# State of a Mamba block in two head halves, its two products as tile pairs of the matmul array

## The chip, the cores and the metric

The program runs on one core of a Trainium2 chip, as one launch. The metric is the device time of that launch in microseconds (us). A core has a matmul engine (TensorE, PE in the profile, with PEld for its weight loads), a vector engine (VectorE, DVE), a scalar engine (ScalarE, ACT), GpSimd (POOL) and a queue that issues transfers (SyncE, SP). They run on their own and wait for each other by semaphores.

## What is computed

Three blocks in a row on 4096 tokens of 256 features: a mixture of experts, a Mamba-2 block, and the same mixture of experts again. The change is in the middle block. Cut to what matters there:

```
zxbcdt = x @ W_in                       # x: layer-normed, (2, 2048, 256)
dt = softplus(dt + dt_bias)             # 8 heads
xBC = silu(conv(xBC) + conv_b)          # causal, 4 taps; x_ssm 8 heads x 64, B 64, C 64
dA = exp(dt * -exp(A_log))
def step(s, inp):                       # s: (batch, 8 heads, 64, 64)
    s = s * dA_t[..., None, None] + dt_t * x_t * B_t
    y = einsum('bhpn,bn->bhp', s, C_t)
    return s, y
y = y + D * x_ssm
y = y * silu(z)
y = y * rsqrt(mean(y * y) + eps) * norm_weight
return y @ W_out
```

## The kernel before

The outer blocks (`ffn_block`, run twice) sort tokens by expert with indirect transfers and are untouched. The middle block is `mamba_block`. It cuts the 4096 tokens into 32 chunks of 128 (T = 32; GC = 4 chunks make a group, 16 chunks make a batch entry). The recurrence is done chunk by chunk: inside a chunk by products with a masked decay matrix, between chunks through a state S.

The order on every engine is written out by hand as a loop over slots, `for s in SLOTS`. In slot s, chunk s gets its state products, chunk s+1 its decay matrix and transposes, chunk s+2 its z projection, chunks s+8 and s+9 their first steps, and chunks s-1 to s-3 their last. Below, "slot i" is the slot in which chunk i gets its state products. Slots differ by k = i mod 4, since the convolution and the softplus of a group of four chunks are laid into certain slots (tables `EARLY`, `LATE`, `TAPPED`, `HANDED`): with k = 3 DVE does the softplus chain of a group ahead, with k = 0 the cumulative sums are made, and with k = 0, 1 and 2 DVE has convolution taps to do. Chunks 28 to 31 have nothing ahead of them.

The steps that the change and the prediction touch, in the order of a slot, with their lines:

- `from_state` (PE, L1323): y from the state, the product of C transposed (CT, 64 partitions by 128 tokens, the weights) with S (64 partitions by 512 columns, 8 heads x 64), into PSUM bank pS. Every fp32 product becomes two weight loads and two matmul instructions on PE ("x2" in the timeline).
- `scale_state` (DVE, L1630): pS times the decay since the chunk's start, into yv.
- `decay_state` (POOL, L1112): S times the decay of the whole chunk. `add_skip` (POOL, L1117) and `gate_y` (POOL, L1122) follow it.
- `out_product` (PE, L1316 with wo): the output projection of chunk i-1; `add_residual` (DVE, L1638) waits for it.
- `within` (PE, L1340): eight products, one for each head, into bank pY; `add_within` (DVE, L1643) adds them to yv.
- `to_state` (PE, L1349): the chunk's contribution to the state, B (in GB, 64 columns of weights) with the weighted x (xt, 128 tokens by 512 columns), again into pS, 64 partitions by 512 columns.
- `turn_b` (PE, L1368) and `turn_xc` (PE, L1376): transposes of the next chunk; in slots with k = 0 `turn_b` waits for DVE's `sum_up` (L1585).
- `new_state` (DVE, L1651): S plus pS. The last chunk of a batch entry sets S to zero instead.
- `silu` (DVE): for the block of channels that holds B and C it runs L1618, which writes C to CT (moved from partitions 64 to 127 down to 0 to 63), and L1619, which does B in place. `gate` (DVE, L1545) gates z and waits for a tanh on ACT.
- ACT makes the exponentials of the sums once for a group (L1267 to L1269), among them ETOT, the chunk decay.
- `softplus` (DVE, from L1569).

Of the kernel before, what the change touches and what calls it, by code (L numbers as in the profile page):

```python
# [883 lines left out]
HANDED = {1: (1, 1), 2: (1, 3)}  # L884
HALO = CONV - 1
RX = 14
LEAD = 10
# [13 lines left out]
def mamba_block(nc, c, keep, early, x, ys_d, conv_w, conv_b, dt_bias, a_log, d_skip, x2, xn_d, batches):  # L901
# [6 lines left out]
    with ExitStack() as ctx:  # L908
# [34 lines left out]
        CT = sb("CT", [NS, 2, GT])  # L943
        S = sb("S", [NS, DIN])
        xt, xdt, xD = (sb(n, [P, DIN]) for n in ("xt", "xdt", "xD"))
# [7 lines left out]

        pT, pP, small, pE, pY, pS, pZ, pO = (ctx.enter_context(nc.psum_tensor(f"bank{n}", [P, 512], F32)) for n in range(8))
        pGB = small[:, 0:P + NS]
# [6 lines left out]
        loads, consts, a_prep, prep = (sem(n) for n in ("m_loads", "m_consts", "a_prep", "m_prep"))  # L962
        soft_chain, tap_chain = sem("soft_chain"), sem("tap_chain")
        x_loaded = [Step(sem(f"x_loaded{n}"), 16) for n in range(4)]
# [115 lines left out]
        def _(pool):  # L1080
# [27 lines left out]
            def decay_state(i):  # L1108
                pool.wait_ge(S_done.sem, S_done.done(i - 1))
                pool.wait_ge(exps.sem, exps.done(i // GC))  # L1110
                pool.wait_ge(i_ready.sem, i_ready.done(i))
                pool.tensor_tensor(by_head(S[:, :]), by_head(S[:, :]), per_head(dts[0:NS, i // GC % 3, ETOT, (i % GC) * H:(i % GC + 1) * H], HD, NS), ALU.mult).then_inc(s1_done.sem, 1)  # L1112

# [51 lines left out]
        def _(act):  # L1165
# [91 lines left out]
            for s in SLOTS:  # L1257
# [7 lines left out]
                if G is not None:  # L1265
                    act.wait_ge(cum_ready.sem, cum_ready.done(G))
                    act.activation(row(G, ECUM), pCum, ACT.Exp)  # L1267
                    act.activation(cumT[0:CH, G % 2, :], pCumT, ACT.Copy)
                    act.activation(row(G, ETOT), pTot, ACT.Exp).then_inc(exps.sem, 1)  # L1269
                if live(s - 3):  # L1270
# [36 lines left out]
        def _(pe):  # L1307
# [11 lines left out]
            def from_state(i):  # L1319
                if i == 0:  # L1320
                    pe.wait_ge(taps.sem, taps.done(NB - 1))
                pe.wait_ge(S_done.sem, S_done.done(i - 1))
                pe.matmul(pS[:, :], CT[:, i // GC % 2, tok(i)], S[:, :], start=True, stop=True).then_inc(i_ready.sem, 1)  # L1323

# [10 lines left out]
            def within(i):  # L1335
                pe.wait_ge(xdt_done.sem, xdt_done.done(i))
                pe.wait_ge(M_done.sem, M_done.done(i))
                pe.wait_ge(t2_done.sem, t2_done.done(i - 1))
                for h in range(H):
# [3 lines left out]
            def to_state(i):  # L1343
                pe.wait_ge(xw_done.sem, xw_done.done(i))
                pe.wait_ge(t1_done.sem, t1_done.done(i))
                if ends(i):
                    pe.sem_inc(s_ready.sem, 1)
                else:
                    pe.matmul(pS[0:NS, :], GB[:, P:P + NS], xt[:, :], start=True, stop=True).then_inc(s_ready.sem, 1)  # L1349

# [130 lines left out]
        def _(dve):  # L1481
# [129 lines left out]
            def silu(G, m):  # L1611
# [5 lines left out]
                else:  # L1617
                    dve.scalar_tensor_tensor(CT[:, q, :], t[NS:P, :], 1.0, a[NS:P, :], ALU.add, ALU.mult)  # L1618
                    dve.scalar_tensor_tensor(a[0:NS, :], t[0:NS, :], 1.0, a[0:NS, :], ALU.add, ALU.mult).then_inc(xc_done.sem, 1)  # L1619

# [4 lines left out]
            def scale_state(i):  # L1625
# [3 lines left out]
                dve.wait_ge(exps.sem, exps.done(i // GC))  # L1629
                dve.tensor_tensor(by_head(yv[:, :]), by_head(pS[:, :]), per_head(row(i // GC, ECUM, i % GC, 1), HD), ALU.mult).then_inc(t1_done.sem, 1)  # L1630

# [8 lines left out]
            def add_within(i):  # L1640
                dve.wait_ge(td_done.sem, td_done.done(i))
                dve.wait_ge(y_ready.sem, y_ready.done(i))
                dve.tensor_tensor(yv[:, :], yv[:, :], pY[:, :], ALU.add).then_inc(t2_done.sem, 1)  # L1643

            def new_state(i):
# [4 lines left out]
                dve.wait_ge(s_ready.sem, s_ready.done(i))  # L1650
                dve.tensor_tensor(S[:, :], S[:, :], pS[0:NS, :], ALU.add).then_inc(S_done.sem, 1)  # L1651

# [94 lines left out]
```

## Time and profile before

| what | us |
|---|---|
| median of three runs | 1271.49 |
| the three runs | 1258.30, 1271.49, 1272.85 |
| span of the profiled execution | 1265.8 |
| median less that span | 5.7 |
| middle block with the state in use (440 to 926) | 486 |

The profiled execution has no time of its own beside its span; the 5.7 us are what stands between its span and the median of the runs. The middle block starts at about 376 us in the trace, its first state product at 440.7 and the last at 902.3.

A row of the timeline reads: start, duration, engine, line, operation, tiles written and read, partitions by columns, and how many equal instructions follow each other (their time together); in brackets how long the engine was idle before and who ended that. Matmul instructions are pipelined and the ends of their records are modelled, so start to start tells more than a record's length.

### The profile page before, as it was taken

To read this page: it belongs to the slowest core of one execution; us is meant where nothing else is said; L and a number is where in the kernel's file an instruction comes from. 1 tells how busy PE (TensorE), PEld (TensorE's weight loads), DVE (VectorE), ACT (ScalarE), POOL (GpSimd) and SP (SyncE) were. 2 spreads that over 40 slices of the span, in tenths; PEclk is the share of its full clock that TensorE was granted. 3 is DMA by queue.
4 is the path that set the end of the run, shared out by engine and by line. 5 is a ranking of instruction groups with operands and counts; after the bars stand their busy time and mean duration, and the time that the engine had idled before them with its cause. 6 is when DMAs were issued, how large, how long until landed. Compare 5 with 4: busy or idle time off the path is not lost. (4 is left out here: it accounts for less than half of the span.)

```text
span 1265.8 us, 21732 instructions
## 1 busy us (share of the span) xinstructions
PE 1050.3 (83%) x6532; PEld 870.1 (69%) x6532; DVE 748.1 (59%) x1614; ACT 605.8 (48%) x1560; POOL 607.9 (48%) x612
## 2 busy tenths in 40 slices
PE   3746999999965788989898888989836999999960
PEld 2745999999954556666676666657525999999950
DVE  5974444444427778677878786865355444444437
ACT  1323555555533455556555656565314555555530
POOL 6922555555531245354545454647502555555520
PEclk9997999999985598899989989999858999999985
DMA  7872222322313101111111110000061232222339
GB/s 227 276 294 74 76 76 76 99 76 76 76 59 93 38 30 43 42 42 42 43 42 42 43 38 17 27 17 21 22 279 38 88 97 92 94 95 91 100 117 327
DMA packets 73258, 112.20 MB, mean 89 GB/s; under 512 B 10680, under 2 KB 60352, under 8 KB 71872
## 3 DMA queue, kind: packets, MB, share of 16 engines
q1 hardware_dynamic: 48704, 60.48, 14.2%
q0 software_dynamic: 13824, 37.77, 9.3%
q10 hardware_dynamic: 10624, 12.58, 2.9%
q8 instruction: 61, 1.00, 0.3%
q14 instruction: 45, 0.37, 0.1%
HBM read 66.76 MB, written 44.04 MB: 88 GB/s over the span
## 5 line engine op out<-in xcount | busy, mean ns | idle before, releaser
L427 POOL DMA_INDIRECT ys_d<-xs,row_of x144 | 142.4, 989 | 195.6 <-DVE xs L811 188.2
L422 POOL DMA_INDIRECT xs<-xn_d,token_of x144 | 140.1, 973 | 115.1 <-DVE token_of L785 71.8
L491 ACT ACTIVATE hs<-pH 128x512 f32<-128x512 f32 x144 | 86.0, 597 | 227.6 <-PE pH L613 217.6
L800 DVE TENSOR_TENSOR xl<-pT,xh 128x256 fp32r<-128x256 f32 x144 | 61.1, 424 | 212.7 <-PE pH L613 108.7
L805 DVE TENSOR_TENSOR h2l<-hs,h2h 128x512 fp32r<-128x512 f32 x144 | 99.8, 693 | 81.3 <-ACT h2h L499 77.3
L1604 DVE SCALAR_TENSOR_TENSOR acc<-bank,cwh,acc 128x511 f32<-128x511 f32 (+2 forms) x120 | 89.6, 747 | 40.5 <-ACT acc L1218 37.7
L633 PE MATMUL pY<-w2h,h2h 128*128 x576 | 103.5, 302 | 1.4 <-DVE h2l L805 1.2
L1122 POOL TENSOR_TENSOR yv<-yv,sz 128x512 f32<-128x512 f32 x32 | 40.7, 1272 | 120.6 <-DVE yv L1643 117.4
L613 PE MATMUL pH<-w1h,xh 128*128 x288 | 93.0, 405 | 1.8 <-DVE xl L800 1.1
L613 PE MATMUL pH<-w1l,xh 128*128 x288 | 92.3, 402 | 0.0
L633 PE MATMUL pY<-w2h,h2l 128*128 x576 | 91.1, 280 | 0.0
L613 PE MATMUL pH<-w1h,xl 128*128 x288 | 90.9, 397 | 0.0
L633 PE MATMUL pY<-w2l,h2h 128*128 x576 | 89.5, 278 | 0.0
L497 ACT ACTIVATE hs<-pR 128x512 f32<-128x512 f32 x144 | 87.3, 606 | 4.2 <-PE pR L622 4.2
L499 ACT ACTIVATE h2h<-pR 128x512 fp32r<-128x512 f32 x144 | 89.0, 618 | 0.0
L622 PE MATMUL pR<-ident,hs 128*128 128x128 f32 x576 | 86.3, 272 | 0.0
L633 PEld LDWEIGHTS pY<-w2h,h2h 128*128 128x128 f32 x576 | 78.2, 190 | 2.5 <-issue 2.5
L1106 POOL TENSOR_TENSOR m_rstd<-m_ve,neghalf 128x3 f32<-128x3 f32 x43 | 41.1, 956 | 76.2 <-DVE m_ve L1533 76.2
L633 PEld LDWEIGHTS pY<-w2h,h2l 128*128 128x128 f32 x576 | 77.5, 188 | 0.0
L633 PEld LDWEIGHTS pY<-w2l,h2h 128*128 128x128 f32 x576 | 76.9, 188 | 0.0
L1316 PE MATMUL bank<-wo,yT 128*128 128x256 f32 x256 | 74.0, 440 | 0.0
L1245 ACT ACTIVATE ex<-bank,dts 128x128 f32<-128x128 f32 x256 | 73.3, 380 | 0.6 <-PE bank L1391 0.6
(250 smaller groups left out, 2591.4 us busy)
## 6 DMA issues: line engine op xcount, KB each, us to landing
m_yg<-ys_d SPq DMA_DIRECT2D x64, 128.0 KB, 2.1
xs<-ys_d SPq DMA_DIRECT2D x12, 512.0 KB, 6.8
wst<-in_L_ffn_w_dram ACTq DMA_DIRECT2D x8, 512.0 KB, 4.6
xs<-in_L_attn_x_dram SPq DMA_DIRECT2D x8, 512.0 KB, 6.5
hs<-in_L_ffn_w_dram ACTq DMA_DIRECT2D x8, 512.0 KB, 4.7
xn_d<-xs SPq DMA_DIRECT2D x8, 512.0 KB, 3.4
lo_d<-w1l SPq DMA_DIRECT2D x1, 4096.0 KB, 11.8
lo_d<-w2l SPq DMA_DIRECT2D x1, 4096.0 KB, 21.4
```

Of the source, the lines that this page charges most:

```text
L422: pool.indirect_dma_start(out=xg[:, t % NX, :], out_offset=None, in_=xn_d, in_offset=bass.IndirectOffsetOnAxis(ap=token_of[:, t:t + 1], ax ...
L427: pool.indirect_dma_start(out=ys_d, out_offset=bass.IndirectOffsetOnAxis(ap=row_of[:, t:t + 1], axis=0), in_=y[:, t % NX, :], in_offset=No ...
L491: act.activation(r[:, u, :], pH[u][:, :], ACT.Relu).then_inc(relu_done.sem, 1)
L497: act.activation(h2[:, u, :, :], turned_h, ACT.Square)
L499: act.activation(h2h[:, u, :, :], turned_h, ACT.Square).then_inc(sq_done.sem, 1)
L613: last = pe.matmul(pH[u][:, :], a[:, u, k, :], w[:, k * HID:(k + 1) * HID], start=(n == 0), stop=(n == 3 * KD - 1))
L622: last = pe.transpose(pR[u][:, k * P:(k + 1) * P], r[:, u, k * P:(k + 1) * P], ident[:, :])
L633: last = pe.matmul(pY[u][:, 0:D], a[:, u, k, :], w[:, k * D:(k + 1) * D], start=(n == 0), stop=(n == 3 * KH - 1))
L805: dve.tensor_tensor(h2l[:, u, :, :], h2[:, u, :, :], h2h[:, u, :, :].bitcast(F32), ALU.subtract).then_inc(h2_split.sem, 1)
L1245: last = act.activation(ex[:, i % 2, h, :], pE[:, n * P:(n + 1) * P], ACT.Exp, bias=dts[:, G % 3, NCUM, k * H + h:k * H + h + 1])
L1316: last = pe.matmul(out, a, b, start=(m == 0), stop=(m == len(parts) - 1))
L1604: ins = dve.scalar_tensor_tensor(a, bank[:, 0:GT - n], cwh[:, b, HALO - n:HALO - n + 1], a, ALU.mult, ALU.add)
```

## The change

S becomes 128 partitions by 256 columns: heads 0 to 3 on partitions 0 to 63, heads 4 to 7 on partitions 64 to 127. `from_state` becomes two products of 64 rows by 256 columns, one in the upper and one in the lower half of the array's rows, into two banks (the first halves of pY and pS, which are now one tensor pYS). `to_state` becomes two products with 64 columns of weights each and 256 columns of data, one in the left and one in the right half of the array's columns, both into the first half of pS. `decay_state` and `new_state` work on 128 by 256 in place of 64 by 512. C is needed on both halves of the partitions, so silu now does C in place too, after it has written CT (a semaphore of its own orders the two). ETOT is laid out by halves, with two instructions on ACT in place of one. Since pY now holds half of the state's product, `from_state` waits for `add_within` of the chunk before (t2), and `within` waits for `scale_state` (t1) of its own chunk.

```diff
+HALF = DIN // 2
+HH = H // 2
...
-        S = sb("S", [NS, DIN])
+        S = sb("S", [P, HALF])
...
+        pYS = ctx.enter_context(nc.psum_tensor("banks45", [P, 2 * 512], F32))
+        pY, pS = pYS[:, 0:512], pYS[:, 512:1024]
+        from_S = pYS[:, :].rearrange("p (b n) -> p b n", b=2)[:, :, 0:HALF].rearrange("p b (h d) -> p b h d", h=HH)
...
-                pool.tensor_tensor(by_head(S[:, :]), by_head(S[:, :]), per_head(dts[0:NS, i // GC % 3, ETOT, (i % GC) * H:(i % GC + 1) * H], HD, NS), ALU.mult).then_inc(s1_done.sem, 1)
+                pool.tensor_tensor(by_head(S[:, :], HH), by_head(S[:, :], HH), per_head(dts[:, i // GC % 3, ETOT, (i % GC) * HH:(i % GC + 1) * HH], HD), ALU.mult).then_inc(s1_done.sem, 1)
...
-                    act.activation(row(G, ETOT), pTot, ACT.Exp).then_inc(exps.sem, 1)
+                    for half in range(2):
+                        at_half = slice(half * NS, (half + 1) * NS)
+                        last = act.activation(by_head(dts[at_half, G % 3, ETOT, 0:GC * HH], GC), by_head(pTot[at_half, :], GC)[:, :, half * HH:(half + 1) * HH], ACT.Exp)
+                    last.then_inc(exps.sem, 1)
...
-                pe.matmul(pS[:, :], CT[:, i // GC % 2, tok(i)], S[:, :], start=True, stop=True).then_inc(i_ready.sem, 1)
+                pe.wait_ge(t2_done.sem, t2_done.done(i - 1))
+                pe.matmul(pYS[:, 0:HALF], CT[:, i // GC % 2, tok(i)], S[0:NS, :], start=True, stop=True)
+                pe.matmul(pYS[:, 512:512 + HALF], acc[NS:P, i // GC % 2, KI, tok(i)], S[NS:P, :], start=True, stop=True).then_inc(i_ready.sem, 1)
...
-                pe.wait_ge(t2_done.sem, t2_done.done(i - 1))
+                pe.wait_ge(t1_done.sem, t1_done.done(i))
...
-                    pe.matmul(pS[0:NS, :], GB[:, P:P + NS], xt[:, :], start=True, stop=True).then_inc(s_ready.sem, 1)
+                    pe.matmul(pS[0:NS, 0:HALF], GB[:, P:P + NS], xt[:, 0:HALF], start=True, stop=True)
+                    pe.matmul(pS[NS:P, 0:HALF], GB[:, P:P + NS], xt[:, HALF:DIN], start=True, stop=True).then_inc(s_ready.sem, 1)
...
-                    dve.scalar_tensor_tensor(CT[:, q, :], t[NS:P, :], 1.0, a[NS:P, :], ALU.add, ALU.mult)
-                    dve.scalar_tensor_tensor(a[0:NS, :], t[0:NS, :], 1.0, a[0:NS, :], ALU.add, ALU.mult).then_inc(xc_done.sem, 1)
+                    dve.scalar_tensor_tensor(CT[:, q, :], t[NS:P, :], 1.0, a[NS:P, :], ALU.add, ALU.mult).then_inc(ct_low, 1)
+                    dve.wait_ge(ct_low, G + 1)
+                    dve.scalar_tensor_tensor(a, t, 1.0, a, ALU.add, ALU.mult).then_inc(xc_done.sem, 1)
...
+                grown = row(i // GC, ECUM, i % GC, 1).rearrange("p (b h a) -> p b h a", b=2, a=1).to_broadcast([P, 2, HH, HD])
+                dve.tensor_tensor(yv[:, :].rearrange("p (b h d) -> p b h d", b=2, h=HH), from_S, grown, ALU.mult).then_inc(t1_done.sem, 1)
...
-                dve.tensor_tensor(S[:, :], S[:, :], pS[0:NS, :], ALU.add).then_inc(S_done.sem, 1)
+                dve.tensor_tensor(S[:, :], S[:, :], pS[:, 0:HALF], ALU.add).then_inc(S_done.sem, 1)
```

On PE, in a slot with k = 0, this stood in a row before (from the state's product to the transposes; semaphore names that the program uses twice stand under their first name, so `e_stored` is the copy of yT):

```order
L1391 MATMUL bank3<-future,ident_bf 128x512
L1323 MATMUL bank5<-S,CT 128x512 [waits m_S]
L1316 MATMUL bank0<-rwT,m_xT2 128x8 [waits m_logit_copied,m_x2T_copied]
L1316 MATMUL bank0<-rwT,m_xT2 128x8
L1316 MATMUL bank7<-wo,yT 128x256 [waits m_xT_lo,e_stored]
L1316 MATMUL bank7<-wo,yT 128x256 x3
L1340 MATMUL bank4<-xdt,ex 128x64 [waits m_t2,m_M,m_xdt]
L1340 MATMUL bank4<-xdt,ex 128x64 x7
L1349 MATMUL bank5<-xt,GB 64x512 [waits m_t1,m_xw]
L1368 MATMUL bank2<-CT,acc 128x128 [waits m_xc,m_dec_in]
```

and on the same engine, at the same place, this now (`s_const` is t2, `res_loaded` the copy of yT):

```order
L1403 MATMUL bank3<-future,ident_bf 128x512
L1333 MATMUL banks45<-S,CT 128x256 [waits s_const,m_S]
L1334 MATMUL banks45<-S,acc 128x256
L1325 MATMUL bank0<-rwT,m_xT2 128x8 [waits m_logit_copied,m_x2T_copied]
L1325 MATMUL bank0<-rwT,m_xT2 128x8
L1325 MATMUL bank7<-wo,yT 128x256 [waits m_xT_lo,res_loaded]
L1325 MATMUL bank7<-wo,yT 128x256 x3
L1351 MATMUL banks45<-xdt,ex 128x64 [waits m_t1,m_M,m_xdt]
L1351 MATMUL banks45<-xdt,ex 128x64 x7
L1360 MATMUL banks45<-xt,GB 64x256 [waits m_t1,m_xw]
L1361 MATMUL banks45<-xt,GB 64x256
L1380 MATMUL bank2<-CT,acc 128x128 [waits m_xc,m_dec_in]
```

The two products each become two, the wait for t2 moves from `within` up to `from_state`, and `within` gets the wait for t1, which `to_state` keeps.

On DVE, at the end of a slot with k = 0, before:

```order
L1550 TENSOR_TENSOR xTl<-bank,xTh 128x2x128 [waits m_xT_hi]
L1618 SCALAR_TENSOR_TENSOR CT<-tb,acc 64x512 [waits m_tb]
L1619 SCALAR_TENSOR_TENSOR acc<-tb,acc 64x512
L1592 TENSOR_TENSOR dts<-dts 128x32 [waits m_dec_out]
L1623 TENSOR_TENSOR ex<-ex,GB 128x1024 [waits m_ex]
```

and on DVE at the same place now:

```order
L1562 TENSOR_TENSOR xTl<-bank,xTh 128x2x128 [waits m_xT_hi]
L1630 SCALAR_TENSOR_TENSOR CT<-tb,acc 64x512 [waits m_tb]
L1632 SCALAR_TENSOR_TENSOR acc<-tb,acc 128x512 [waits ct_low]
L1604 TENSOR_TENSOR dts<-dts 128x32 [waits m_dec_out]
L1636 TENSOR_TENSOR ex<-ex,GB 128x1024 [waits m_ex]
```

Nothing moved there; the second instruction is twice as tall and waits for the first.

## Rows read from the trace of the kernel before

**Rows 1.** The page, its head and part 1: the head line and the busy time of each engine.

```profile
span 1265.8 us, 21732 instructions
...
PE 1050.3 (83%) x6532; PEld 870.1 (69%) x6532; DVE 748.1 (59%) x1614; ACT 605.8 (48%) x1560; POOL 607.9 (48%) x612
```

**Rows 2.** The windows by stage: length, busy time of each engine (instructions), granted clock, DMA share, GB/s.

```profile
core 0: us, PE busy (x) PEld busy (x) DVE busy (x) ACT busy (x) POOL busy (x), PEclk, DMA share, GB/s
...
440.00:926.00 486.00, 432.08 (x2352) 315.49 (x2351) 342.80 (x717) 271.73 (x809) 250.15 (x250) 0.94 0.11 34
```

**Rows 3.** The view of tile S, whole run: duration in ns, least, median and greatest; first and last start.

```profile
L1323 PE MATMUL bank<-S,CT x64: 589/693/1057, 440.7 to 902.9; 64*128 64x512 f32 x64
L1112 POOL TENSOR_TENSOR S<-S,dts x30: 1032/1036/1340, 442.0 to 893.8; 64x512 f32<-64x512 f32 x30
L1651 DVE TENSOR_TENSOR S<-S,bank x30: 669/672/680, 448.3 to 898.2; 64x512 f32<-64x512 f32 x30
```

**Rows 4.** The view of waits, middle block: who waited for whom, us in total, times, longest.

```profile
DVE xo L1638 <- PE bank L1316: 28.8, 17, 6.3
...
DVE yv L1630 <- PE bank L1323: 4.5, 7, 1.0
...
DVE S L1651 <- PE bank L1349: 2.8, 6, 1.2
```

**Rows 5.** The timeline of PE in slot 27: start us, us, engine, line, operation, tiles.

```profile
859.04 1.12 PE L1323 MATMUL bank<-S,CT 64*128 64x512 f32 x2
...
860.56 1.97 PE L1316 MATMUL bank<-wo,yT 128*128 128x256 f32 x8
862.37 1.89 PE L1340 MATMUL bank<-xdt,ex 128*128 128x64 f32 x16
864.19 1.07 PE L1349 MATMUL bank<-xt,GB 128*64 128x512 f32 x2
865.19 0.48 PE L1368 MATMUL bank<-CT,acc 64*128 64x128 f32 x2
```

**Rows 6.** The timeline of PE in slot 8.

```profile
570.27 1.12 PE L1323 MATMUL bank<-S,CT 64*128 64x512 f32 x2
...
571.95 3.49 PE L1316 MATMUL bank<-wo,yT 128*128 128x256 f32 x8
...
577.10 1.07 PE L1349 MATMUL bank<-xt,GB 128*64 128x512 f32 x2
578.10 0.49 PE L1368 MATMUL bank<-CT,acc 64*128 64x128 f32 x2
```

**Rows 7.** The timeline of DVE in slot 8.

```profile
577.73 0.19 DVE L1585 TENSOR_TENSOR dts<-bank,dts 128x32 f32<-128x32 f32 x1
```

**Rows 8.** The windows, a stretch of slot 8; columns as in group 2.

```profile
571.70:574.90 3.20, 3.20 (x10) 2.66 (x10) 2.96 (x5) 1.23 (x5) 2.13 (x2) 0.50 0.00 0
```

**Rows 9.** The timeline of PE in slot 10.

```profile
607.26 1.89 PE L1340 MATMUL bank<-xdt,ex 128*128 128x64 f32 x16
```

**Rows 10.** The timeline of DVE in slot 10.

```profile
606.21 0.68 DVE L1630 TENSOR_TENSOR yv<-bank,dts 128x512 f32<-128x512 f32 x1
...
611.77 0.67 DVE L1643 TENSOR_TENSOR yv<-yv,bank 128x512 f32<-128x512 f32 x1
```

**Rows 11.** The timeline of DVE in slot 7.

```profile
562.23 0.67 DVE L1651 TENSOR_TENSOR S<-S,bank 64x512 f32<-64x512 f32 x1
562.82 0.93 DVE L1569 TENSOR_SCALAR dts<-dts 128x32 f32<-128x32 f32 x1
```

**Rows 12.** The timeline of POOL in slot 7.

```profile
562.45 1.27 POOL L1122 TENSOR_TENSOR yv<-yv,sz 128x512 f32<-128x512 f32 x1 [2.93 <-DVE yv L1643]
```

**Rows 13.** The timeline of DVE at the end of slot 8.

```profile
585.83 0.68 DVE L1619 SCALAR_TENSOR_TENSOR acc<-tb,acc 64x512 f32<-64x512 f32 x1
...
589.16 0.69 DVE L1545 SCALAR_TENSOR_TENSOR sz<-tz,bank 128x512 f32<-128x512 f32 x1 [1.41 <-ACT tz L1200]
```

**Rows 14.** The timeline of ACT in slot 8.

```profile
570.18 0.17 ACT L1269 ACTIVATE dts<-bank 128x32 f32<-128x32 f32 x1
```

More of the change, by code:

```diff
@@ L952, in mamba_block @@
         DTR, DPOS, DABS, DU, DS, DS2, DQ, DT, DA, NCUM, ECUM, DEC, DECDT, ETOT = range(NR)
-        pT, pP, small, pE, pY, pS, pZ, pO = (ctx.enter_context(nc.psum_tensor(f"bank{n}", [P, 512], F32)) for n in range(8))
+        pT, pP, small, pE = (ctx.enter_context(nc.psum_tensor(f"bank{n}", [P, 512], F32)) for n in range(4))
+        pYS = ctx.enter_context(nc.psum_tensor("banks45", [P, 2 * 512], F32))
+        pZ, pO = (ctx.enter_context(nc.psum_tensor(f"bank{n}", [P, 512], F32)) for n in (6, 7))
+        pY, pS = pYS[:, 0:512], pYS[:, 512:1024]
+        from_S = pYS[:, :].rearrange("p (b n) -> p b n", b=2)[:, :, 0:HALF].rearrange("p b (h d) -> p b h d", h=HH)
         pGB = small[:, 0:P + NS]
@@ L962, in mamba_block @@
         loads, consts, a_prep, prep = (sem(n) for n in ("m_loads", "m_consts", "a_prep", "m_prep"))
-        soft_chain, tap_chain = sem("soft_chain"), sem("tap_chain")
+        soft_chain, tap_chain, ct_low = sem("soft_chain"), sem("tap_chain"), sem("ct_low")
         x_loaded = [Step(sem(f"x_loaded{n}"), 16) for n in range(4)]
@@ L1629, in scale_state @@
                 dve.wait_ge(exps.sem, exps.done(i // GC))
-                dve.tensor_tensor(by_head(yv[:, :]), by_head(pS[:, :]), per_head(row(i // GC, ECUM, i % GC, 1), HD), ALU.mult).then_inc(t1_done.sem, 1)
+                grown = row(i // GC, ECUM, i % GC, 1).rearrange("p (b h a) -> p b h a", b=2, a=1).to_broadcast([P, 2, HH, HD])
+                dve.tensor_tensor(yv[:, :].rearrange("p (b h d) -> p b h d", b=2, h=HH), from_S, grown, ALU.mult).then_inc(t1_done.sem, 1)
             def add_residual(s):
@@ L1642, in add_within @@
                 dve.wait_ge(y_ready.sem, y_ready.done(i))
-                dve.tensor_tensor(yv[:, :], yv[:, :], pY[:, :], ALU.add).then_inc(t2_done.sem, 1)
+                dve.tensor_tensor(yv[:, :], yv[:, :], pY, ALU.add).then_inc(t2_done.sem, 1)
             def new_state(i):
```

## The prediction

> **What bounds the kernel now.** I read the page first. Its chain of waits ends in the last block and doesn't reach into the middle one, and part 1 only says that PE is the busiest engine at 83% of a span of 1265.8 us [rows 1]. The windows by stage come next: the middle block with its state takes 486 us, PE is busy in 432 of them (89%), DVE in 343, POOL in 250 [rows 2]. No engine there is full, so I went through the timeline slot by slot and asked at each idle time who ended it.
>
> Three kinds of slot come out. In slots 27 to 30 PE runs from the state's product to the next one almost without a pause; slot 27 stands for them [rows 5]. In slots with k = 0 PE leads from `from_state` through `out_product`, `within` and `to_state` to the transposes, with DVE close behind [rows 6, 7]. In slots with k = 3 PE leads as far as `out_product`, and then DVE does, since `add_residual` waits for it. In most slots with k = 1 and 2 DVE leads: it is late with convolution taps, `within` is long done when `add_within` begins, and PE has time in hand [rows 9, 10].
>
> To count the slots in which `from_state` is on the path I used the view of waits. DVE's `add_residual` waits for `out_product` 17 times (28.8 us) [rows 4]; one of these is behind the last `from_state`, and slot 31 has the other late one, so 16 slots. `scale_state` waits for `from_state` 7 times [rows 4], five of them in slots already counted; the two new ones are slots 16 and 24. That makes **18 of 32 slots for `from_state`**. `new_state` waits for `to_state` only 6 times [rows 4]: slots 4, 13 and 27 to 30.
>
> **The change part by part.**
>
> *`from_state`.* The price of a pass comes from slot 27: `out_product` is eight instructions of 256 columns, and from its start to that of `within` are 862.37 - 860.56 = 1.81 us, so 0.226 us a pass of 256 columns [rows 5]. `to_state`, two passes of 512 columns, takes 865.19 - 864.19 = 1.00 us from its start to that of `turn_b` [rows 5]: four times 0.226 plus 0.10 for coming in and going out. `from_state` has the same two passes (a record of 1.12 us against 1.07). After the change there are four passes of 256 columns: upper half first pass, upper half second pass, lower half first, lower half second. The same 0.90 us of streaming remains if nothing overlaps. Passes on one half of the array can't overlap each other, so in this order only the second pass of the first product and the first pass of the second one can. That leaves three passes in a row and saves 0.226 us. Ends of the range: nothing saved (four passes one after another), and 0.45 us (both products side by side in both passes). The trace before has no two neighbouring products in different halves, so no row decides. I take the middle because the order of the four passes allows just that.
>
> Sum: 18 slots x 0.226 = 4.1 us, and two of the slots (4 and 31) ran with PE at the lower clock (the longest record of `from_state` is 1057 ns against a median of 693 [rows 3]), where a pass costs double: + 0.45. So **4.5 us**, between 0 and 9.
>
> *`to_state`.* It is fully on the path in the 6 slots above: 6 x 0.226 = 1.36, and 0.23 more for slot 4 at the lower clock, so 1.6 us. In slots 8, 12, 20 and 24 the saving meets DVE: `turn_b` starts at 578.10 and DVE's sums, for which it waits, end at 577.73 + 0.19 = 577.92 [rows 6, 7]. Only 0.18 us can be saved there, 4 x 0.15 = 0.6 us. Sum **2.2 us**, between 0 and 4. Both ends are bounds by rows: a product can't save more than half of its passes.
>
> *`new_state`.* From 672 ns [rows 3] to about 0.40 us, by half of its columns. It has no worth where it looks as if it had: in slots with k = 3 it stands before the softplus chain, but the first instruction of that chain (L1569, 562.82, 0.93 us for 32 columns) ends at 563.75, just when POOL's `gate_y` ends (562.45 + 1.27 = 563.72) [rows 11, 12]. The small instruction is held by POOL's; if it starts 0.27 us sooner, it ends at the same time. Elsewhere DVE waits after it. **0 us**, at most 5 x 0.27 = 1.3 us.
>
> *`decay_state`.* From 1036 ns for 512 columns [rows 3] to something above half. POOL then starts `add_skip` sooner, but `gate_y` waits 2.93 us for `add_within` [rows 12]. 0 us.
>
> *ACT.* One more instruction of some 0.17 us [rows 14] in eight slots. ACT ends ETOT at 570.18 + 0.17 = 570.35, and the first reader waits for `from_state`, which starts at 570.27 and runs over a microsecond [rows 6]. Even with `from_state` shorter, 0.5 us are left. 0 us.
>
> *silu.* The in-place half grows from 64 to 128 partitions, which by the forms of DVE's rows is no longer in time, and waits for the one before it. It ended at 586.51, and DVE next waited 1.41 us for ACT's tanh [rows 13], with only two instructions of its own in between. 0 us; without that cover it would be some 0.1 us in each of eight slots.
>
> *The moved waits.* `from_state` now waits for t2 of the chunk before, but DVE does that before the `S_done` it waits for anyway: 0. `within` now waits for t1. Behind it in PE's queue stand `to_state` and the transposes. In slot 27 it starts at 862.37; `scale_state` is done well before it, since two PE products stand between. In slot 10 the rows show the tight case: `scale_state` ends at 606.21 + 0.68 = 606.89 and `within` starts at 607.26, 0.37 us later [rows 9, 10]. With `from_state` shorter by 0.23 us it comes as near as 0.14 us, and some such slots will see `within` held by one or two tenths. But these are the slots in which DVE starts `add_within` at 611.77, more than 2.5 us after `within` ended (607.26 + 1.89 = 609.15) [rows 9, 10]. 0 us.
>
> **Sum:** 4.5 + 2.2 = 6.7 us; some of it is lost where DVE or ACT comes next within two tenths, so I take **6 us** off the profiled 1265.8. That stands 5.7 us under the median of the runs. From the median: 1271.5 - 6 = **1265.5 us**.
>
> **The rivals.** *(B) The pairs run one after another.* Four passes of 256 columns take what two of 512 took; the 6.7 us are 0, and two more instructions cost some hundredths. 1271.5, up to 1273. For it: the array must get data for two fp32 products at once, and no row shows that it can. Against it: upper and lower half read different partitions, at least in `from_state`.
>
> *(C) Both products run side by side from the first pass on.* 0.45 us a pair: 9 + 3.8 us, less what DVE takes back, 1260. Against it: the second product stands behind both passes of the first. The Trainium skill, TensorEngine Tiling (Array Packing), Theoretical Speedup, gives up to 2x for a small dimension of 64 or less, and under Key Properties it says that different tiles can load weights and multiply in parallel; by that page the sum would be this case's. No run here shows it.
>
> *(D) Slower: the clock.* The granted clock was 0.94 in the mean of the block [rows 2], 1.0 in most slots, and 0.50 (1.2 GHz) in a stretch of slot 8, just after PE had waited for the softplus chain [rows 8]. `out_product` took 3.49 us there against 1.97 in slot 27 [rows 5, 6], so such a stretch on the path costs 1.5 us. The change takes work off PE and lengthens its waits. Four more stretches eat the 6 us; from five on the kernel is slower; ten would give 1265.5 + 15 = 1280. Against it: PE loses 0.45 us of some 13.5 busy us a slot. The three runs before already lie 14.5 us apart, which such stretches can explain, though one trace can't show it.
>
> *(E) The change loses its gain at the other engines*, because DVE and ACT lead right behind PE: a gain of 2 us, 1269.5. It lies between the forecast and (B).
>
> **How the numbers follow.** Chances: forecast 0.42, (B) 0.22, (C) 0.10, (D) 0.14, (E) 0.12. The prediction is the likeliest, 1265.5 us. The range takes in the ends of the two unknown prices (1260 to 1273) and the few us that the median of such runs moves by itself; it leaves out the faster end of (C) in a low median and the far part of (D): 1256 to 1277. A change of 2% (25 us) is about what a measurement of this kernel can tell from none. It would take the whole of the two products and `new_state` off the path, or seventeen slow stretches more: faster 0.03, same 0.93, slower 0.04.
>
> **What the profile after will show.** If I am right, `from_state` to the next product takes some 0.85 us in place of 1.05 in unhurried slots, the third of its four matmul records starts with the second, and slots 27 to 30 are shorter by 0.45 us each. Under (B) their length stays. `new_state` falls to 0.4 us with the softplus chain no sooner done. The number of slow-clock stretches in the block tells (D). I am wrong if `within` is held in slots with k = 0 or 3, or if the lower half's product waits for the whole of the upper's and adds a weight load of its own.

## The result and the profile after

The changed kernel takes **1250.24 us** (median of 13 runs, 1247.15 to 1252.44). The kernel before takes 1262.42 us (median of 13 runs, 1257.38 to 1272.85). The ratio is 0.9882, 95% interval 0.9853 to 0.9911: 12 us, 1.2%, faster, which is clear of the noise but less than the 2% from which the prediction speaks of faster. The time lies outside the predicted range of 1256 to 1277. The median of three runs from which the prediction counted down, 1271.49, is 9.1 us above that of the thirteen. The kernel before moves from session to session: in the four later ones its median was 1272.04, 1268.54, 1267.81 and 1271.20 us. The changed kernel's was 1252.38 in the one of them in which it ran again, so it lies under 1256 from either base.

The profiled run took 1250.99 us, its span is 1249.3 us, so 1.7 us lie around a span. The head and part 1 of its page, against [rows 1]:

```profile
span 1249.3 us, 22019 instructions
...
PE 1015.9 (81%) x6656; PEld 861.7 (69%) x6656; DVE 736.6 (59%) x1614; ACT 606.7 (49%) x1568; POOL 596.5 (48%) x612
```

The middle block by windows, from the first `from_state` to the last (columns as in [rows 2]), of the kernel after, then of the one before:

```profile
438.40:886.10 447.70, 387.15 (x2407) 298.96 (x2406) 329.44 (x703) 265.89 (x797) 230.61 (x245) 0.96 0.11 36
```

```profile
440.70:902.30 461.60, 414.13 (x2285) 302.46 (x2284) 337.43 (x703) 265.96 (x794) 243.44 (x245) 0.95 0.11 35
```

That stretch is 13.9 us shorter. The spans differ by 16.5; 2.3 of the other 2.6 us lie ahead of the first state product, in code that the change doesn't touch. PE in slot 27 of the kernel after, against [rows 5]:

```profile
846.17 0.48 PE L1333 MATMUL banks<-S,CT 64*128 64x256 f32 x1
846.18 0.48 PE L1334 MATMUL banks<-S,acc 64*128 64x256 f32 x1
846.50 0.38 PE L1333 MATMUL banks<-S,CT 64*128 64x256 f32 x1
846.50 0.38 PE L1334 MATMUL banks<-S,acc 64*128 64x256 f32 x1
846.81 0.61 PE L1325 MATMUL bank<-rwT,m_xT 128*128 128x8 f32 x4
847.27 1.97 PE L1325 MATMUL bank<-wo,yT 128*128 128x256 f32 x8
849.09 1.89 PE L1351 MATMUL banks<-xdt,ex 128*128 128x64 f32 x16
850.91 0.43 PE L1360 MATMUL banks<-xt,GB 128*64 128x256 f32 x1
850.92 0.43 PE L1361 MATMUL banks<-xt,GB 128*64 128x256 f32 x1
851.18 0.38 PE L1360 MATMUL banks<-xt,GB 128*64 128x256 f32 x1
851.18 0.38 PE L1361 MATMUL banks<-xt,GB 128*64 128x256 f32 x1
851.49 0.48 PE L1380 MATMUL bank<-CT,acc 64*128 64x128 f32 x2
```

and there before, ahead of the rows in [rows 5] the product that follows `from_state`:

```profile
859.04 1.12 PE L1323 MATMUL bank<-S,CT 64*128 64x512 f32 x2
860.09 0.61 PE L1316 MATMUL bank<-rwT,m_xT 128*128 128x8 f32 x4
```

Look at the order of the starts. The kernel's source has the whole upper product (both passes) and then the whole lower one. The records have upper, lower (0.01 us behind), upper, lower. Both pairs do this. (The records tell when an instruction started, not its place in the built program. So whether the engine or the build put the passes in turn isn't shown; what is shown is that they ran side by side.) From `from_state` to the next product are 846.81 - 846.17 = 0.64 us, against 860.09 - 859.04 = 1.05 before; from `to_state` to `turn_b` 0.58 against 1.00. Each pair saves about 0.42 us, nearly half of the 0.90 us of passes that the prediction counted. The Trainium skill (TensorEngine Tiling (Array Packing), Key Properties) says that different tiles can load weights and multiply in parallel; these records agree, in fp32, for halves of the rows and for halves of the columns.

The lengths of the slots (start of one `from_state` to the next, from the timelines, us), the kernels of two experiments beside them; * marks a slot in which the granted clock fell to 0.5 (1.2 GHz) for a while:

| slot | before | after | `f_twice` | `t_twice` |
|---|---|---|---|---|
| 4 (k=0) | 22.04* | 17.50* | 18.54* | 21.65* |
| 5, 17 (k=1) | 15.85 | 15.86 | 15.86 | 15.85, 15.86 |
| 7, 19 (k=3) | 15.12 | 14.51 | 14.94 | 14.72, 14.71 |
| 8 (k=0) | 17.27* | 15.91 | 16.34 | 15.90 |
| 16 (k=0) | 16.37 | 15.95 | 16.39 | 15.96 |
| 18 (k=2) | 14.84* | 14.84* | 14.67* | 14.84* |
| 24 (k=0) | 14.96 | 14.21 | 17.82* | 16.22* |
| 28 | 10.93 | 10.09 | 10.53 | 10.53 |

Eighteen slots (1, 5, 7, 9, 11, 15 to 17, 19, 21 to 25, 27 to 30) ran wholly at 2.4 GHz in both profiles, and they are together 7.6 us shorter: 0.84 in each of slots 27 to 30, 0.61 in slots 7, 11 and 19, 0.42 in slot 16, and nothing in most slots with k = 1. That is the change itself. The other thirteen aren't comparable, as one or both had such a stretch. Five of them, slots 3, 4, 8, 12 and 20, are of kinds in which the pair counts; at 0.42 each, an estimate, they add 2.1. So about **9.7 us** are the change's, and the other 4 us of the 13.9 are the clock. It took as well as gave: slots 10 and 14 ran at full clock before and are 1.59 and 1.58 us longer after. In sum, between the state products of chunks 1 and 31 the records of the granted clock add up to 41.0 us at 1.2 GHz before and 27.3 after.

In slots with k = 0, `to_state` ends sooner for nothing, since `turn_b` waits for DVE's sums. PE in slot 8, against [rows 6]:

```profile
569.04 0.38 PE L1360 MATMUL banks<-xt,GB 128*64 128x256 f32 x1
569.05 0.38 PE L1361 MATMUL banks<-xt,GB 128*64 128x256 f32 x1
570.51 0.49 PE L1380 MATMUL bank<-CT,acc 64*128 64x128 f32 x2 [1.08 <-DVE dts L1597]
```

In slots with k = 3 the block runs on DVE's softplus chain, which shares its pace with POOL. POOL and DVE in slot 7 of the kernel after, against [rows 11, 12]:

```profile
556.42 1.27 POOL L1128 TENSOR_TENSOR yv<-yv,sz 128x512 f32<-128x512 f32 x1 [2.94 <-DVE yv L1657]
557.65 1.04 POOL L1136 TENSOR_TENSOR xdt<-xt,dts 128x512 f32<-128x512 f32 x1
```

```profile
556.19 0.41 DVE L1665 TENSOR_TENSOR S<-S,banks 128x256 f32<-128x256 f32 x1
556.52 1.20 DVE L1581 TENSOR_SCALAR dts<-dts 128x32 f32<-128x32 f32 x1
...
558.14 0.59 DVE L1583 TENSOR_TENSOR dts<-dts 128x32 f32<-128x32 f32 x1
```

and POOL and DVE there before:

```profile
563.87 1.04 POOL L1130 TENSOR_TENSOR xdt<-xt,dts 128x512 f32<-128x512 f32 x1
```

```profile
564.18 0.78 DVE L1571 TENSOR_TENSOR dts<-dts 128x32 f32<-128x32 f32 x1
```

`new_state` fell from 672 to 414 ns, and the chain's first instruction grew from 0.93 to 1.20 us: it ends at 557.72, with POOL's `gate_y` (556.42 + 1.27 = 557.69). So `new_state`'s gain is worth nothing, as predicted. But POOL's next instruction, the one that scales x, started 0.15 us after `gate_y` before (563.87 against 563.72) and starts at once now. It reads xt, which comes out of the transposes behind `to_state`. DVE's third instruction of the chain ends with it (564.96 against 564.91 before, 558.73 against 558.69 after), and so `to_state` shortens slots with k = 3 by 0.19 us (0.61 less the 0.42 of `from_state`), which the prediction hadn't seen. `t_twice` below bears it out: a second pair of `to_state` costs 0.21 us in slot 7.

### The profile page after: what moved, and what is told of

Same layout as the page of the kernel before. It is cut to its first block and busy times, and to the rows that moved or that the text cites. A ratio compares the mean times of both kernels' runs of the same rounds, so it can differ in the third digit from the quotient of the medians.

```text
span 1249.3 us, 22019 instructions
## 1 busy us (share of the span) xinstructions
PE 1015.9 (81%) x6656; PEld 861.7 (69%) x6656; DVE 736.6 (59%) x1614; ACT 606.7 (49%) x1568; POOL 596.5 (48%) x612
## 5 line engine op out<-in xcount | busy, mean ns | idle before, releaser
L1616 DVE SCALAR_TENSOR_TENSOR acc<-bank,cwh,acc 128x511 f32<-128x511 f32 (+2 forms) x111 | 82.9, 747 | 41.9 <-ACT acc L1224 39.3
L1351 PEld LDWEIGHTS banks<-xdt,ex 128*128 128x128 f32 x512 | 64.8, 200 | 5.6 <-issue 4.3
```

What stands on the lines that cost most here:

```text
L1351: last = pe.matmul(pY[:, h * HD:(h + 1) * HD], ex[:, i % 2, h, :], xdt[:, h * HD:(h + 1) * HD], start=True, stop=True)
L1616: ins = dve.scalar_tensor_tensor(a, bank[:, 0:GT - n], cwh[:, b, HALO - n:HALO - n + 1], a, ALU.mult, ALU.add)
```

## The experiments

All are edits of the changed kernel unless it says otherwise. Times are medians; "before" is the kernel before on the same chip. Its median changed by up to 9.6 us between sessions and the changed kernel's by 2.1, so a ratio to before doesn't compare one experiment with another: `f_twice` has the changed kernel's ratio, though its slots are longer. The comparisons with the changed kernel go by the times and by the lengths of the slots. Of a pair the "upper" product is L1333, the "lower" L1334.

**1. What are the pairs worth?** Three kernels pull the two products of a pair apart. `f_apart` runs the lower half of `from_state` behind `project_dt` and `score`, ahead of `out_product`; `t_apart` runs the left half of `to_state` ahead of `within`; `both_apart` does both.

```diff
+            def from_lower(i):
                 pe.matmul(pYS[:, 512:512 + HALF], acc[NS:P, ...
...
                 if live(s - 3):
                     score(s - 3)
+                if live(s):
+                    from_lower(s)
...
                 if live(s):
+                    to_left(s)
                     within(s)
                     to_state(s)
```

> The changed kernel with the two products of from_state pulled apart: the lower half comes after project_dt and score in PE's order, to_state stays a pair. Theory P (each pair runs side by side in all its passes and saves 0.42 us where PE leads): from_state's share comes back, 0.42 us plus some 0.1 to 0.2 us for the added changes between row halves and whole array, in 18 slots: 8 to 11 us slower than the changed kernel (1250), so 1258 to 1261, about the kernel before. Theory V (the gain is the shorter work on DVE and POOL): no change, 1250. Theory K (the gain is mostly fewer stretches at the lower clock): no change beyond 2 us, and stretches as in the changed kernel.

> The changed kernel with the two products of to_state pulled apart: the left half comes ahead of the eight products of within, the right half behind them; from_state stays a pair. Theory P: 0.42 us plus 0.1 to 0.2 us in slots 13 and 27 to 30, and part of it (0.2 us) in slots with k = 3, nothing in slots with k = 0, where PE waits 1.08 us for DVE behind to_state: 3 to 5 us slower than the changed kernel, 1253 to 1255. Theory V and theory K: no change, 1250.

> The changed kernel with both pairs pulled apart: the new layout of the state and the shorter work on DVE and POOL stay, no two halves stand side by side. Theory P: the whole gain of 10 to 12 us goes and the added changes of mode cost 2 to 5 us more: 1262 to 1267. Theory V: 1250. Theory K: 1250 to 1255.

Measured: `t_apart` 1254.56 us (ratio to before 0.9884, 0.9851 to 0.9917), in the range expected; slots 28 and 29 took 10.85 and 10.86. `f_apart` 1281.31 us (1.009, 1.0058 to 1.0122) and `both_apart` 1280.92 us (1.0094, 1.006 to 1.0129), above their expectations by 20 and 14 us. In the tail `f_apart` took 10.80, so the pair there gives 0.42 and keeping away from other products some 0.3. The 0.3 is what is left over, not measured by itself. `both_apart` took 11.57 or 11.58 us in slots 27 to 29: the two losses add up. It has the shorter `decay_state` and `new_state` too, and its tail is longer than the 10.93 before, so those two aren't the gain there.

`t_apart`'s total was in the range partly by luck. Its left half stands ahead of `within`, so `within` starts 0.58 us later. PE in slot 7:

```profile
549.65 0.65 PE L1358 MATMUL banks<-xt,GB 128*64 128x256 f32 x2
550.23 2.00 PE L1351 MATMUL banks<-xdt,ex 128*128 128x64 f32 x16
552.16 0.65 PE L1366 MATMUL banks<-xt,GB 128*64 128x256 f32 x2
```

`add_within`, `gate_y` and the softplus chain then come later, and slots 7 and 19 took 15.57 us against 14.51, where 0.2 had been expected. Against that, slots 6, 14, 18 and 26 had no stretch at 1.2 GHz and were 1.6 us shorter each (slots 8, 12 and 20 had one instead). So `t_apart` doesn't measure the pair of `to_state` alone either.

The rest of `f_apart`'s excess came from where the half was put. PE in `f_apart`, two lines of slot 26, then slot 27:

```profile
859.75 0.61 PE L1325 MATMUL bank<-rwT,m_xT 128*128 128x8 f32 x4 [0.67 <-ACT m_xT L1194]
860.28 0.70 PE L1336 MATMUL banks<-S,acc 64*128 64x256 f32 x2
...
871.61 0.70 PE L1333 MATMUL banks<-S,CT 64*128 64x256 f32 x2
872.23 0.61 PE L1325 MATMUL bank<-rwT,m_xT 128*128 128x8 f32 x4
872.77 0.70 PE L1336 MATMUL banks<-S,acc 64*128 64x256 f32 x2
```

One product alone takes 872.23 - 871.61 = 0.62 us from start to start; the pair took 0.64. **The second product of a pair is free.** And the lower half stood behind `score`'s wait for ACT, which the first line shows. `scale_state` waited for it 16 times in the middle block, 17.2 us together, against twice and 0.8 us in the changed kernel:

```profile
DVE yv L1648 <- PE banks L1336: 17.2, 16, 2.7
```

```profile
DVE yv L1644 <- PE banks L1334: 0.8, 2, 0.5
```

Slots with k = 1 went from 15.86 to 17.2 us, and the time at 1.2 GHz from 27.3 to 64.9 us. `f_apart` therefore doesn't measure the pair.

**2. The same without that wait.** `f_around` runs the upper half ahead of the first `sums` and the lower half behind it, so that nothing between them waits.

> The changed kernel with from_state's upper half ahead of the five products of sums and its lower half behind them, so that no wait is put between the halves that was not ahead of from_state before (in the run with the halves around project_dt and score, the lower half stood behind score's wait for ACT, and the time rose by 30 us instead of 8 to 11). Theory P: the overlap of one pair goes (0.42 us) and one or two changes between row halves and whole array come on top (0.1 to 0.3 us): slots 27 to 30 take 10.6 to 10.8 us instead of 10.09, the whole 8 to 13 us more than the changed kernel, 1258 to 1263.

Measured: 1275.47 us (1263.13 to 1286.92), ratio 1.0034 (0.9999 to 1.007). The tail is as expected, 10.82, but the total is 12 us over the expectation. Slots 5 and 13 took 21.7 and 21.2 us. The window over slot 5, with the granted clock at 0.69, and the same window in `around_warm`, which is `f_around` with the idle-time matmuls of experiment 6:

```profile
519.00:541.00 22.00, 20.66 (x92) 15.96 (x91) 12.32 (x25) 11.22 (x33) 7.06 (x7) 0.69 0.09 31
```

```profile
519.00:541.00 22.00, 21.61 (x141) 17.32 (x141) 15.60 (x30) 13.60 (x42) 8.92 (x9) 1.00 0.10 31
```

> The kernel with from_state's halves on either side of sums, with the idle matmuls of warm_after. If the 25 us that f_around lost against the changed kernel are 12 us of passes and mode changes and the rest clock, the fill takes the rest away: 1258 to 1264, with the long spells at 1.2 GHz in slots 5 and 13 gone. If the loss is in PE's order itself, it stays at 1270 or above.

`around_warm` took 1260.8 us (0.9945, 0.9908 to 0.9983), as expected; slots 5 and 13 were back at 15.86 and 15.07. Those two slots alone are 12.5 us of `f_around`'s time. So its excess over the expectation was the clock.

**3. How many slots is each product on the path of?** `f_twice` runs the pair of `from_state` twice, `t_twice` that of `to_state`.

```diff
                 pe.matmul(pYS[:, 0:HALF], CT[...], S[0:NS, :], ...)
+                pe.matmul(pYS[:, 512:512 + HALF], acc[NS:P, ...], S[NS:P, :], ...)
+                pe.matmul(pYS[:, 0:HALF], CT[...], S[0:NS, :], ...)
                 pe.matmul(pYS[:, 512:512 + HALF], acc[NS:P, ...], S[NS:P, :], ...).then_inc(i_ready.sem, 1)
```

> The changed kernel with the pair of from_state issued twice (the second overwrites the same values). Theory P: one pair more is 0.43 us of PE, in 18 slots on the path: 7 to 8 us slower than the changed kernel, 1257 to 1259. If a pair ran one product after the other it would be 0.85 us in 18 slots, 15 us, 1265. Theory V: the same as P by the side of PE, so it only tells the count of slots; if DVE set the time everywhere, no change.

> The changed kernel with the pair of to_state issued twice. Theory P: 0.43 us more in slots 13 and 27 to 30, some 0.2 to 0.4 us in slots with k = 3, nothing in slots with k = 0 (1.08 us of idle PE behind it): 3 to 5 us slower, 1253 to 1255. If to_state counted in all slots where from_state does, 7 to 8 us, 1258.

Measured: `f_twice` 1256.16 us (0.9885, 0.985 to 0.9919), a little under the expectation; `t_twice` 1259.23 us (0.9913, 0.9879 to 0.9946), 4 us over. By the table above, a second pair costs 0.43 to 0.44. `from_state`'s is paid in the twelve slots 7, 8, 11, 12, 16, 19, 20, 27 to 30, and 15 with 0.50 (0.09 in slot 23). `to_state`'s is paid in slots 27 to 30 (0.82 in slot 27, which isn't explained), 0.31 in slot 25, 0.2 in slots 7, 11 and 19, and not at all in slots 8, 12, 13, 16 and 20. `t_twice`'s total is above `f_twice`'s for another reason: slots 4 and 24 took 21.65 and 16.22 us, with stretches at 1.2 GHz.

**4. Is it the pairing, or only the cut into 256 columns?** `b_split` is the kernel before with both products cut in two of 256 columns, on the same half of the array.

> The kernel before, with from_state and to_state each as two products of 256 columns on the same half of the array (same rows, same columns of the array, one bank). Nothing can overlap if the halves are what matters: slots 27 to 30 stay at 10.93 us (at most 0.05 more) and the time that of the kernel before. If two shorter products in place of one were the gain, 10.1 us and 10 us less than before.

Measured: 1263.49 us (0.9986, 0.995 to 1.0022), tail 10.94 against 10.93. PE in slot 27:

```profile
863.74 0.70 PE L1323 MATMUL bank<-S,CT 64*128 64x256 f32 x2
864.28 0.59 PE L1324 MATMUL bank<-S,CT 64*128 64x256 f32 x2
864.80 0.39 PE L1316 MATMUL bank<-rwT,m_xT 128*128 128x8 f32 x2
```

Two products on one half take 1.06 us; the cut alone gives nothing.

**5. Must two neighbours lie in different halves?** `q_uull` runs `from_state` as four products of 128 columns, upper, upper, lower, lower; `q_ulul` alternates them.

```diff
+                for n, (half, part) in enumerate(((0, 0), (0, 1), (1, 0), (1, 1))):
+                    a = (CT[...], acc[NS:P, ...])[half]
+                    last = pe.matmul(pYS[:, half * 512 + part * P:...], a, S[half * NS:(half + 1) * NS, part * P:(part + 1) * P], ...)
```

> The changed kernel with from_state in four products of 128 columns in the order upper, upper, lower, lower. It tells how far the engine looks for a product of the other half. If only neighbours pair up and starts keep the order, the second upper and the first lower run together, half of the overlap is lost: slots 27 to 30 take 10.09 + 0.21 = 10.3 us. If the halves are independent queues, 10.1 us.

> The changed kernel with from_state in four products of 128 columns in the order upper, lower, upper, lower. Neighbours lie in different halves: the overlap of the changed kernel is kept, slots 27 to 30 at 10.1 us (up to 0.1 more for four more weight loads), 1250 to 1252.

Measured: 1253.83 us (0.9883, 0.9836 to 0.9931) and 1252.37 us (0.9881, 0.9836 to 0.9927), tails 10.11 and 10.11. PE in slot 27 of `q_uull`:

```profile
858.45 0.37 PE L1335 MATMUL banks<-S,CT 64*128 64x128 f32 x1
858.46 0.37 PE L1335 MATMUL banks<-S,acc 64*128 64x128 f32 x1
858.66 0.27 PE L1335 MATMUL banks<-S,CT 64*128 64x128 f32 x1
858.67 0.27 PE L1335 MATMUL banks<-S,acc 64*128 64x128 f32 x1
858.77 0.27 PE L1335 MATMUL banks<-S,CT 64*128 64x128 f32 x1
858.78 0.27 PE L1335 MATMUL banks<-S,acc 64*128 64x128 f32 x1
858.88 0.27 PE L1335 MATMUL banks<-S,CT 64*128 64x128 f32 x1
858.89 0.27 PE L1335 MATMUL banks<-S,acc 64*128 64x128 f32 x1
```

The first lower product (acc) starts with the first upper one (CT), though the source has two upper products, four passes, ahead of it. The theory that only neighbours overlap, with a tail of 10.3, falls. The Trainium skill (TensorE: Matmul & The Clock Gate, The mechanism) says that matmuls start and end in the order of the program; between halves of the array these records show otherwise, unless the build had already put the passes in turn, which no run here tells. The length of the slots goes with the records.

**6. What does the clock do to all this?** Across 70 runs of the kernel before on three chips, time and mean granted clock go together: from 1258.0 us at 0.930 to 1276.6 us at 0.909, 8.0 us for 0.01, correlation -0.94. `warm_before` and `warm_after` add idle-time matmuls to the two kernels where PE waits: seven ahead of `turn_y` in slots with k = 2, six ahead of the late projections with k = 0 and 1, five ahead of the cumulative sums. They write banks that are free at that time, and nothing reads them.

```diff
+            def fill(bank, n):
+                for _ in range(n):
+                    pe.matmul(bank[:, 0:P], ident[:, :], c["ones_f"][:, :], start=True, stop=True)
...
+                    if s % GC == 2 and live(s + 2):
+                        pe.wait_ge(sz_done.sem, sz_done.done(s + 1))
+                        fill(pZ, 7)
                     turn_y(s)
...
+                if s % GC < 2 and live(s) and live(s + GC):
+                    pe.wait_ge(S_done.sem, S_done.done(s))
+                    fill(pS, 6)
```

> The kernel before with the same idle matmuls. With the clock evened out in both, what stands between this one and warm_after is the change itself. Theory P: 10 us (1254 here against 1244). Theory K: 2 us or less. The run before had more and longer stretches at the lower clock than the changed kernel, so this one should gain more from the fill: 5 to 10 us below 1262.

> The changed kernel with idle matmuls of constants where PE waits (seven before turn_y in slots with k = 2, six before the late projections with k = 0 and 1, five before the cumulative sums with k = 3), into banks that are free there; no result changes. Theory K: the stretches at 1.2 GHz between 480 and 860 us (five in this trace that cost 1.6 us each) go, 5 to 8 us faster where the fill stays inside the waits: 1243 to 1246. Theory P says nothing against that; if a stretch costs nothing where it lies, no change, 1250, or up to 5 us slower where the fill runs over.

Measured: `warm_before` 1256.05 us (0.9898, 0.986 to 0.9937), `warm_after` 1248.74 us (0.9829, 0.9789 to 0.9868). The kernel before gains 12.5 us from work that computes nothing. `warm_after` had been expected at 1243 to 1246 us and gained less: 13.7 us at 1.2 GHz are left in its profile after the first slot, in slots 3, 8, 12 and 20, the last three of which took 17.41, 17.04 and 17.53. `warm2_before` and `warm2_after` add four more ahead of `turn_y` with k = 3 and four ahead of `turn_b` with k = 0; `after_again` is the changed kernel as it is, on the same chip.

> The kernel before with the same fuller fill. Theory P with the clock as an addition: it stands 8 to 11 us above warm2_after, 1254 to 1258. If the change's gain were mostly clock, the two would meet within 3 us.

> The changed kernel with the idle matmuls of warm_after and more of them where the trace of warm_after still showed PE idle ahead of a stretch at 1.2 GHz: four before turn_y with k = 3, four before turn_b with k = 0. If the clock is what is left to gain, the stretches in slots 8, 12 and 20 (1.2 to 1.5 us each) go: 2 to 5 us faster than the changed kernel, 1245 to 1248. If the fill only takes PE's time, 1250 or slower.

> The changed kernel itself once more, on the same chip and among the same runs of the kernel before as the other three. 1247 to 1253, with a mean granted clock of 0.922 to 0.928; the ratio to before 0.983 to 0.991.

Measured: `warm2_before` 1257.08 us (0.9911, 0.9881 to 0.9942), `warm2_after` **1242.99 us** (0.9793, 0.9751 to 0.9836), `after_again` 1252.38 us (0.9859, 0.9812 to 0.9907; five runs lie between 1249.09 and 1254.21, with a median of 1252.20, and a sixth took 5395 us). `warm2_after` is the fastest kernel of this study, 9.4 us under the changed kernel on the same chip, where 2 to 5 had been expected. The windows from 438 to 888 of `warm2_after`, then of `after_again`:

```profile
438.00:888.00 450.00, 426.06 (x2849) 347.04 (x2877) 337.38 (x711) 267.18 (x802) 236.37 (x248) 0.99 0.12 36
```

```profile
438.00:888.00 450.00, 383.32 (x2392) 298.84 (x2421) 332.07 (x707) 267.22 (x805) 230.69 (x246) 0.96 0.11 36
```

PE is busy 43 us longer, and the kernel is faster. With the fuller fill in both, 0 and 3.4 us at 1.2 GHz are left after the first slot, and the change can be read with the clock nearly evened out. From the first to the last `from_state` the profiles have 452.67 against 442.88 us, 9.8 less. (The medians can't be used for it: those of `warm_before` and `warm_after` stand 7.3 us apart, those of `warm2_before` and `warm2_after` 14.1, and the runs of `warm2_before` spread from 1252.58 to 1262.08, the profiled one being the fastest.) In five of the slots with k = 0 the fill ahead of `turn_b` costs the kernel before some 0.37 us (slot 16: 16.74 against 16.37) that the changed kernel hides in its wait. The other way round, in slots 7 and 19 the fill costs the changed kernel 1.06 us and the one before 0.9, and slot 13 of `warm2_after` has a stretch at 1.2 GHz. So 8 to 10 us are the change's, an estimate, which fits the 9.7 from the slots.

**7. Is `new_state` really worth nothing?** `dve_more` puts its gain back: one more DVE instruction of 128 columns from PSUM ahead of `new_state`, 0.28 us.

> The changed kernel with 0.28 us put back on DVE ahead of new_state in every slot (a sum of a constant and 128 columns of the state's bank, into a spare tile), so that it is as long as before. My account (the shorter new_state is hidden, since the softplus chain is held by POOL and elsewhere DVE waits): no change, 1250, at most 1 us. Theory V: a third or more of the gain comes back, 1254 or above.

Measured: 1251.12 us (0.9853, 0.9818 to 0.9889), slots 7, 16 and 28 at 14.52, 15.97 and 10.09 us against 14.51, 15.95 and 10.09. The shorter `new_state` is worth nothing.

## Why the prediction was wrong

**The step that failed** is in *`from_state`*: "Passes on one half of the array can't overlap each other, so in this order only the second pass of the first product and the first pass of the second one can." The first half of that holds (`b_split`). The second doesn't: all passes of the two halves overlap, though the source has them in another order, and a pair saves 0.42 us, not 0.226 (`q_uull` against `q_ulul`, and the timeline after). That was rival (C)'s mechanism, which had 0.10. The argument against it, that the second product stands behind both passes of the first, was the same unmeasured belief. The page cited under (C) was right. (C)'s number, 1260, was still 10 us high: it had 0.45 us in too many slots and nothing for the clock, and that its 11.5 us lie near the measured 12.2 is luck.

**How much of the miss is which.** The forecast was 15.3 us too high: 9.1 for its base and 6.2 for the change. By the profiles, whose spans differ by 16.5 us where 6 was forecast, the 10.5 more are some 3.7 from the pairs, some 4 from the clock and 2.6 outside the stretch with the state. So the failed step, with the count of slots below, accounts for about a quarter of the miss.

**The number of slots.** The prediction had `from_state` on the path in 18 slots; `f_twice` shows it fully paid in 12 (0.50 in slot 15 among them), and the clock hides slots 0, 3, 4 and 24 there. Slot 24, at full clock before and after, is 0.75 us shorter. In the pair with the clock evened out, slot 3 is 0.43 shorter, slot 4 0.78 (0.37 of it the fill's) and slot 0 only 0.11. That makes 15. At 0.226 us that is 3.4 us, not 4.1. For `to_state`, slots 27 to 30 were right and slot 13 isn't borne out: `t_twice` costs 0.01 us there. Slots 8, 12 and 20 were rightly held by DVE's sums, and the 0.15 us given to each isn't seen: slot 16, of the same kind and at full clock, is 0.42 shorter, which `from_state` alone gives. The path through xt and POOL to the softplus chain, 0.19 us in slots with k = 3, was missed. Put together, 15 times 0.42 is 6.3, `to_state` gives four times 0.42 and three times 0.19, 2.3, and the sum is 8.6 us, an estimate, near the 9.7 of the slots and within the 8 to 10 of the evened pair. That the forecast's 2.2 us for `to_state` comes out is luck: a price too low, in more slots.

**The base.** The measured median of the kernel before is 1262.42, not 1271.49. The profiled span of 1265.8 us, with the 1.7 us around it that the later profiles have, is a run of about 1267.5 us, so the 5.7 us between span and median were no constant of the kernel but one run against others. Counted from there, its own 6 us give 1261.5. But 1271.49 wasn't odd either, as the medians of the later sessions show (1267.81 to 1272.04), and the changed kernel's 1252.38 beside 1271.20 was outside the range too.

**(D), the clock**, went the other way: 41.0 us at 1.2 GHz before, 27.3 after, worth some 4 us to the change. The 1.5 us for one stretch were about right with k = 2 and high with k = 0: slots 10, 14 and 26 with one are 1.6 us longer than the same slots without (14.87 against 13.28, 14.11 against 12.53, 13.80 against 12.22), while slots 8 and 20 with one took 17.27 and 17.32, slot 16 without one 16.37, 0.9 us less. "Seventeen more" to reach 2% slower was counted without the 6 us gained; with them it is 21. What wasn't seen is how far they can go in one slot: slot 4 took 22.04, 17.50, 18.54 and 21.65 us in four kernels. Why the stretches begin in just these slots isn't settled; no run here varied one gap alone.

**What held.** `new_state` was worth 0 (`dve_more`), with the softplus chain's first instruction ending when POOL's `gate_y` does. `decay_state` fell to 614 ns and POOL then waited 2.94 us as before. `within` waits for t1 in some slots with k = 1 and 2, and in slot 0, and starts 0.15 us after `scale_state` ends; with the clock evened out slots 2, 6, 10 and 18 kept their length (13.20, 13.27, 13.29 and 13.27 us). Slot 0, with k = 0, is the one place where the prediction's own sign of being wrong came up; it took 17.37 us against 17.48 there, so it cost nothing. The view of tile S shows the sizes:

```profile
L1118 POOL TENSOR_TENSOR S<-S,dts x30: 606/614/827, 439.3 to 878.5; 128x256 f32<-128x256 f32 x30
L1665 DVE TENSOR_TENSOR S<-S,banks x30: 401/414/417, 445.2 to 882.0; 128x256 f32<-128x256 f32 x30
```

## What to carry to other kernels

An fp32 product that uses 64 rows or 64 columns of the array can be cut in two halves that run side by side, and here 0.42 of some 1.0 us was gone. The pair has to stand together: with other products in between, even where nothing waits (`f_around`), the overlap was lost. Inside the group of row halves the order made no difference; for column halves it wasn't tried. Price such a saving by doubling the operation, not by counting waits alone: `f_twice` told in one run which slots pay, except those that the clock hid. And where the runs of one kernel lie 15 us apart, look at the granted clock first: fill PE's waits in both kernels and compare those.

## What the runs showed of the hardware

- Two halves of the array took their products out of the order of the source: in `q_uull` the third product started 0.01 us after the first. With the starts in the order of the source the tail slots were expected at 10.3 us; they took 10.11, as with alternating halves. A pair (0.64 us) costs what one of its products costs alone (0.62 us).
- A product alone between products of other shapes took 0.62 us, two in a row on one half 1.06 together: 0.09 us each for standing alone.
- Matmuls that compute nothing, put into PE's waits, took 12.5 us off the kernel before (`warm_before`) and 9.4 us off the changed one (`warm2_after`, granted clock 0.99 in the block against 0.96). The stretches at 1.2 GHz belong to the schedule: the changed kernel on chip 3 (`after_again`), `dve_more` on chip 13 and `q_uull` on chip 6 all have them in slots 0, 3, 4, 6, 10, 14, 18 and 26, 23.9 us in each after the first slot.
- A DVE instruction of 32 columns (SBUF to SBUF) lasted 0.93 us beside one POOL instruction and 1.20 us when it began 0.27 us sooner: it ended with POOL's both times.
